# Edge passes of an attention layer in chunks of 32 steps instead of 16, with rings of 64 places and new engine orders

## The reference

```
h = relu(layernorm(x));  x = x + sage(h)      # two layers: mean of h[src] per dst, then dense, log_softmax
h = relu(layernorm(x));  x = x + attention(h) # two layers:
    q, k, v = h@Wq+bq, h@Wk+bk, h@Wv+bv       # 4 heads of 32
    e = edge_weight @ We
    alpha = sum(q[dst] * (k[src] + e)) / sqrt(32)          # per edge and head
    a = softmax of alpha over the edges of one dst
    out = segment_sum((v[src] + e) * a, dst)
    h = h + relu(batchnorm(gate(out, h@Wskip+bskip)))
```

## Time and profile before

| | |
|---|---|
| median of 3 runs | 9833.48 us (9824.3 to 9843.5) |
| profiled execution | 9827.85 us, its span 9826.1 us |
| busy share | POOL 66%, DVE 57%, PE 55%, ACT 30% |
| gathers | 6656, POOL, L537 and L1138 |
| DMA moved | 1053.31 MB, mean 107 GB/s |

### The profile page before, as it was taken

One profiled execution on the slowest core, in us unless ns is written; L12 is line 12 of the kernel. 1 busy time (PEld: TensorE's weight loads), 2 busy tenths in 40 slices (PEclk: granted clock), 3 DMA queues, 4 the chain that ended last, 5 costly groups with the idle time before them and its releaser, 6 DMA issues. The chain is left out here.

```text
span 9826.1 us, 135707 instructions
## 1 busy us (share of the span) xinstructions
PE 5382.9 (55%) x24088; PEld 4490.4 (46%) x24088; DVE 5601.9 (57%) x17532; ACT 2975.7 (30%) x6690; POOL 6499.9 (66%) x6729
## 2 busy tenths in 40 slices
PE   1444444447444444443367677777656777767774
PEld 1333333335333333332156566666525666656663
DVE  4333333332333333334777777777767777777776
ACT  2000000002000000000246666666524666666663
POOL 4777777772577777775067777777605777777770
PEclk8555555558655555555777777777777777777777
DMA  5222222222222222222355555555435555555553
GB/s 118 53 52 53 53 52 53 53 53 76 62 53 53 53 52 53 53 53 56 116 162 161 159 159 159 161 160 161 136 125 165 159 159 154 159 159 160 160 149 105
DMA packets 648320, 1053.31 MB, mean 107 GB/s; under 512 B 287942, under 2 KB 445894, under 8 KB 621528
## 3 DMA queue, kind: packets, MB, share of 16 engines
q0 software_dynamic: 268320, 659.00, 24.7%
q1 hardware_dynamic: 286552, 323.24, 10.6%
q10 hardware_dynamic: 93408, 70.66, 2.2%
HBM read 974.79 MB, written 77.54 MB: 107 GB/s over the span
## 5 line engine op out<-in xcount | busy, mean ns | idle before, releaser
L1138 POOL DMA_INDIRECT conv_kv<-key_value,conv_src x3328 | 3265.7, 981 | 1698.6 <-issue 968.2
L537 POOL DMA_INDIRECT second_msg<-sage_hidden_projected,second_src x1664 | 1586.8, 954 | 749.8 <-issue 506.8
L537 POOL DMA_INDIRECT first_msg<-sage_in,first_src x1664 | 1585.2, 953 | 559.3 <-issue 506.8
L1394 PE MATMUL conv_ps_sums<-conv_pv,conv_sel 128*128 128x136 f32 x6656 | 1511.6, 386 | 396.8 <-DVE conv_pv L1197 209.5
L594 PE MATMUL first_ps_sums<-first_msg,first_sel 128*128 128x129 f32 x3328 | 858.4, 439 | 1258.3 <-DVE first_sel L548 907.6
L594 PE MATMUL second_ps_sums<-second_msg,second_sel 128*128 128x129 f32 x3328 | 858.4, 439 | 1250.4 <-DVE second_sel L548 907.3
L1394 PEld LDWEIGHTS conv_ps_sums<-conv_pv,conv_sel 128*128 128x128 f32 x6656 | 1258.8, 270 | 583.7 <-issue 310.1
L1375 PE MATMUL conv_ps_query<-query_table,conv_selT 128*128 x6656 | 1331.6, 363 | 75.0 <-issue 61.5
L594 PEld LDWEIGHTS first_ps_sums<-first_msg,first_sel 128*128 128x128 f32 x3328 | 745.2, 329 | 1371.4 <-DVE first_sel L548 989.3
L594 PEld LDWEIGHTS second_ps_sums<-second_msg,second_sel 128*128 128x128 f32 x3328 | 745.1, 329 | 1363.8 <-DVE second_sel L548 989.0
L1375 PEld LDWEIGHTS conv_ps_query<-query_table,conv_selT 128*128 128x128 f32 x6656 | 1174.8, 262 | 96.4 <-issue 78.8
(11 more groups left out here) (210 smaller groups left out, 5443.7 us busy)
## 6 DMA issues: line engine op xcount, KB each, us to landing
conv_place<-place_rows SPq DMA_DIRECT2D x208, 1024.0 KB
conv_kv<-key_value,conv_src POOLq DMA_INDIRECT x3328
first_msg<-sage_in,first_src POOLq DMA_INDIRECT x1664, 2.5
second_msg<-sage_hidden_projected,second_src POOLq DMA_INDIRECT x1664, 2.5
key_value<-project_kv ACTq DMA_DIRECT2D x28, 896.0 KB
conv_pen<-run_penalties SPq DMA_DIRECT2D x832, 24.2 KB
project_hT<-conv_in_transposed SPq DMA_DIRECT2D x28, 448.0 KB
combine_hT<-conv_in_transposed SPq DMA_DIRECT2D x28, 448.0 KB
```

The lines of the kernel that those rows point to most:

```text
L537: pool.indirect_dma_start(msg[:, (b % 2) * CH + j, 0:D], None, table, bass.IndirectOffsetOnAxis(ap=src[:, b, j:j + 1], axis=0)).then_inc(g ...
L1138: pool.indirect_dma_start(kv[:, h * CH + j, :], None, t.kv_d, bass.IndirectOffsetOnAxis(ap=src[:, h, j:j + 1], axis=0)).then_inc(gathered[ ...
L1394: last = pe.matmul(sums_of(step), sel[:, h * CH + step, :], pv[:, step, :, :].rearrange("p h w -> p (h w)"), start=True, stop=True)
```

## The change

CH becomes 32: 52 chunks of 8 groups, rings of 64 places, HR = 128 rows in the tiles of the softmax chain. This holds for the `sage_edges` passes too, whose code is not changed otherwise. In `conv_edges`:

- `multiply` writes the products over the keys in `kv`, `weigh` writes over the values in `kv`, and the softmax weights and the weighted edge weights go to the last 8 of the 128 key columns, so that PE's operand of 136 columns is a piece of `kv`. `prod` and `pv` are gone. The order of the 136 columns of the sums changes, and `conv_combine` and `rescaled` (now two operations) with it.
- `away` and `awayT` are gone: ACT works in place in `sel` and `selT`, which are now rings of 4 groups.
- `place` is loaded in four pieces of 512 KB per chunk of 32; `rec` is split into `wd` (weights and dead marks) and `rel` (the node of each edge), each with a load of its own.
- POOL may reuse a place only when PE's sums of it are done (`sums_ready`).
- DVE's order: `stages(a, b)` has first the softmax of the older chunk b, with the scores of three groups of the newer chunk a in its gaps (`fill`), then all eight `weigh` with `rescaled` after the first, then five sections, each with multiply, edge term and score sum of one group of a, and 6 or 7 adds of b. Block numbers are read 16 at a time, twice per chunk. The orders of PE, ACT and SP follow.

```diff
-CH = 16
+CH = 32
+SELG = 4
+NEAR = 3
+DEN = D - 2 * HEADS
+ADDS = (0, 7, 14, 20, 26, CH)
+PAIRS_OF = ((0, 4), (4, 7), (7, 10), (10, 13), (13, KP))
...
                         for k in range(KG):
-                            pool.wait_ge(pv_ready, KG * c + k + 1)
+                            pool.wait_ge(sums_ready, KP * c + 2 * k + 2)
...
+                def scores(a, k):
+                    m = multiply(a, k)
+                    edge_term(a, k)
+                    need(m)
+                    score_sum(a, k)
...
+                    values = slots(h, k)[:, :, D:2 * D].rearrange("p i (h c) -> p i h c", h=HEADS)
+                    dve.tensor_tensor(values, values, bc(slots(h, k)[:, :, DEN:DEN + HEADS], 3, [P, GR, HEADS, C]),
                                       ALU.mult).then_inc(pv_ready, 1)
...
+                def blocks_of(b, half):
+                    c, h, g = b
+                    if half == 0:
+                        dve.wait_ge(blk_in[h], 16 * g + 16)
+                        dve.sem_inc(go_v, 1)
+                    dve.load(regs, blk[0:1, h, half * (CH // 2):(half + 1) * (CH // 2)])
...
+                    at = softmax(b, fill)
+                    weigh(b, 0)
+                    before[0] = rescaled(b, at)
+                    for k in range(1, KG):
+                        weigh(b, k)
+                    for k in range(NEAR, KG):
+                        if a is not None:
+                            m = multiply(a, k)
+                            edge_term(a, k)
+                        lo, hi = ADDS[k - NEAR], ADDS[k - NEAR + 1]
+                        for step in range(lo, hi):
+                            if step == CH // 2:
+                                at = blocks_of(b, 1)
+                            add(step, at)
+                            if step == lo and a is not None:
+                                need(m)
+                                score_sum(a, k)
...
+                    for k in range(NEAR, KG):
+                        if a is not None:
+                            if k == KG // 2:
+                                at = blocks_of(a, 1)
+                            queries(a, k, at)
+                        sums(b, *PAIRS_OF[k - NEAR])
                     if following is not None:
-                        queries(following, 2, at)
-                    return at
+                        queries(following, 0, blocks_of(following, 0))
```

More of the change, by code:

```diff
@@ L1109, in _, with places @@
             def _(sp):
+                flat = t.place_d.rearrange("c n -> (c n)")
+                steps = t.b_d.rearrange("c n -> (c n)")
+                def places(c, h, g, q):
+                    sp.wait_ge(place_used, 4 * c + q + 1)
+                    sp.dma_start(place[:, q % 2, :], flat[bass.ds(c * (CH * P) + q * (2 * GR * P), 2 * GR * P)]
+                                 .partition_broadcast(P)).then_inc(place_in[q % 2], 16)
                 with sp.Fori(0, PAIRS) as g:
@@ new lines, in softmax @@
+                def softmax(b, fill):
+                    c, h, g = b
+                    step = [stp[:, h, :, n] for n in range(HK)]
+                    near = score[:, h, :, :]
+                    dve.wait_ge(q_used, KG * c + KG + 2)
+                    need(chain.n)
+                    m = mark(dve.tensor_tensor(near, near, qwe[:, :, :], ALU.add))
+                    need(m)
+                    dve.tensor_tensor(near, near, bc(wd[:, h, 1, :], 1, [P, HEADS, CH]), ALU.add).then_inc(scored, 1)
+                    fill(0)
@@ L1351, in _, with stages, add, fill @@
-                stages(chunk(PAIRS - 1, 1), chunk(PAIRS - 1, 0), None)
-                stages(None, chunk(PAIRS - 1, 1), None)
+                    dve.sem_inc(wd_used, 1)
+                    return at
+                def stages(a, b):
+                    c, h, g = b
+                    before = [None]
+                    def add(step, at):
+                        j = step // PAIR
+                        if step % PAIR == 0:
+                            dve.wait_ge(sums_ready, KP * c + (j + 1 + 2 * KP))
+                        if step > 0 and step % PAIR == 0:
+                            dve.wait_ge(ps_used, KP * c + (j + 2))
+                        else:
+                            need(before[0])
+                        acc = t.acc[:, bass.ds(at[step % (CH // 2)] * AW, AW)]
+                        ins = dve.tensor_tensor(acc, acc, sums_of(h, step), ALU.add)
+                        if step % PAIR < PAIR - 1:
+                            before[0] = mark(ins)
+                        else:
+                            ins.then_inc(ps_used, 1)
+                    def fill(k):
+                        if a is not None:
+                            scores(a, k)
+                    at = softmax(b, fill)
[13 more added lines that the diff above has]
+                            if step == lo and a is not None:
+                                need(m)
+                                score_sum(a, k)
@@ L1354, in _ @@
+                for k in range(KG):
+                    scores(chunk(0, 0), k)
+                stages(chunk(0, 1), chunk(0, 0))
+                with chain.turns(PAIRS - 1, 2 * (2 * KG + 15 + KP)) as g:
+                    stages(chunk(g + 1, 0), chunk(g, 1))
+                    stages(chunk(g + 1, 1), chunk(g + 1, 0))
+                stages(None, chunk(PAIRS - 1, 1))
             @block.tensor
             def _(pe):
-                pe.sem_inc(q_ready, KG)
+                pe.sem_inc(q_ready, SELG)
@@ L1368, in loaded, with blocks_of @@
                     return [pe.snap(r, min_val=0, max_val=NB - 1) for r in regs]
+                def blocks_of(a, half):
+                    c, h, g = a
+                    if half == 0:
+                        pe.wait_ge(blk_in[h], 16 * g + 16)
+                        pe.sem_inc(go_t, 1)
+                    pe.load(regs, blk[0:1, h, half * (CH // 2):(half + 1) * (CH // 2)])
+                    return loaded()
                 def queries(a, k, at):
@@ L1409, in stages @@
                     pe.wait_ge(scored, c + 1 + 2)
                     pe.sem_inc(go_t, 1)
-                    pe.transpose(rows, score[:, :, :].rearrange("p h t -> p (h t)"), t.ident[:, :]).then_inc(rows_ready, 1)
-                    sums(b, (6,))
+                    pe.transpose(rows, score[:, h, :, :].rearrange("p h t -> p (h t)"), t.ident[:, :]).then_inc(rows_ready, 1)
+                    if a is not None:
+                        queries(a, 1, at)
                     pe.wait_ge(ends_ready, c + 1)
```

363 lines of the change are left out of this document (138 added, 225 removed).

## The result

The changed kernel takes 9773.67 us (9765.26 to 9781.53, 4 runs) where the kernel before takes 9834.67 (9824.3 to 9843.5, 4 runs): a ratio of 0.9939, interval 0.9925 to 0.9952, 61 us faster. A second comparison gave 9775.52 us against 9824.89, 0.9949 (0.9935 to 0.9964). The profiled execution took 9781.53 us, the slowest of its four; its span is 9779.8 us, 46.3 us less than the span before, where the medians differ by 61.

A forecast was written before the change was run, and what follows sets the result against it. The prediction took POOL's gather pace to bound all four passes. Held gathers at -26 us and ends of passes at +26 us, all else 0, summed to no change: 9833 us, range 9775 to 9900.

The forecast's parts named there:

- The frame: All four edge passes: POOL's pace of 1.25 us a gather sets them, 1664 gathers or 2080 us a pass.
- Held gathers: Conv passes: gathers held by DVE operations with two SBUF inputs fall from 120.7 to 95 us, -26 us.
- the distance of 1.815 us: Row of weighs: from a held gather's release to the next start, landing where it just escapes or is caught for 0.5 us.
- Rival A: Conv passes: gathers mostly escape at the seams of the eight weighs, 0.45 us a chunk, -48 us, 9785 us; chance 0.29.
- Ends of passes: Conv passes' ends: the last chunk's work lies open, about +13 us a pass, +26 us for two.
- DVE's turn: DVE's work for 32 steps: 36.5 us, 4 us shorter than POOL's 40.9, so its saving is worth 0.
- rival B: Conv passes: DVE and PE become the bound; a turn of 43 us gives 10080 us, 41.5 us gives +90; chance 0.15.
- Starts: Starts of passes: the first gather's wait for the src load and that load's wait for DVE's clearing both stay, 0.
- SP's queue: SP's loads: same place bytes in half-size pieces, half as many small tables of twice the size, issued early enough, 0.
- the new condition of POOL: POOL's place reuse: `sums_ready` replaces `pv_ready`, yet each place is free 19 to 32 us ahead, 0.
- Sage passes: Sage passes: DVE groups meeting gathers come half as often but behind a 32-register load, between -14 and +14 us, taken as 0.
- Rival C: Conv passes: gathers are caught in step with DVE's weighs, 1.4 us a chunk, +51 us, 9885 us; chance 0.18.

The follow-up runs named there:

- i1: Kernel before, with `weigh` and L548 each reading one input from PSUM and the fourth weigh moved ahead of the last two score operations: 9688.16 us, ratio 0.9864.
- g4: Kernel before, with all four weighs of a chunk in a row at its head, nothing else altered: 9754.55 us, ratio 0.9926.
- g2: Changed kernel, with each score sum of a conv pass done twice, the second into an unread tile: 10053.01 us, ratio 1.023 to the kernel before.
- g1: Changed kernel with nothing altered, run again beside the kernel before on one chip: 9775.52 us, ratio 0.9949.
- g3: Kernel before, with each score sum of a conv pass done twice, the second into an unread tile: 9797.13 us, ratio 0.9971.

## Why the prediction was wrong

*The frame held.* POOL's pace sets the passes: the gathers became 78.1 us shorter and the conv passes 77.4 us; i1 forecast 136 us from lengthened gathers alone and measured 135.

*The step that failed is "Held gathers", -26 us where -78 was measured.* The mechanism was right, its size was not. I had the one catch and the distance of 1.815 us = 3 x 0.604 that puts the next gather on a seam. I then let that gather be "just caught" for a part of the phases, and took the one behind it, 2 x 0.604 = 1.208 against 1.25 us, to start 0.04 us into a weigh and lose 0.5 us. That gave 0.73 us for a row of seven. The row loses 0.18 us. What I didn't know is who gives way at a seam: DVE does, by 0.04 us, and so the next gather meets a seam too. 104 rows x 0.55 us = 57 us, against the 52 by which the term was off (95 forecast, 42.6 measured; the other operations hold gathers for 0.05 us a chunk more than I gave them). The trace of before had this: its 40 gathers within 0.02 us of a weigh's start lost nothing. I didn't look for them, and priced positions at random where the earlier trace rows could have been asked gather by gather. Rival A, at 0.29, was the true one; its 0.45 us a chunk is 0.41 as measured (42.6 / 104).

*Ends of passes, +26:* 38.3 us for 38, and +27.6 in the two gaps behind the conv passes. Right. g4 shows what that costs: 21 us between two kernels with the same gathers.

*DVE's turn, 36.5 us and 4 us of slack:* too short. The slack was 2.0 us, by g2, so the turn is 38.4 us. The first register load stops DVE 1.6 us (ahead of L1257) and not 0.65: the load itself takes 1.10 us in both kernels, but in the kernel before it runs beside two weighs that DVE already has, and here beside nothing. And ahead of L1226, the first operation of each turn of the loop, DVE stops for 3.3 us or so in "issue", 24 times in 1950 us:

```profile
6029.44 0.29 DVE L1226 TENSOR_TENSOR conv_score<-conv_score,conv_qwe 128x128 f32<-128x128 f32 x1 [3.37 <-issue]
```

That is 1.6 us a chunk. The two are more than the 1.9 us that the sum lacks, so other terms of it were too long; they weren't measured one by one. In the kernel before no such row stands, and the instruction queue moved 30 packets, 0.25 MB, where it now moves 428. The records of DVE's sequencer place the stop: it lies between the loop's branch and the next instruction, 3.2 us in the median where the kernel before has 0.23, and in each of the 48 stops of the two passes a packet of the instruction queue starts within the first 2.5 us. This is what rival B's sentence on the doubled loop bodies spoke of; what the Trainium skill says of taken branches (Runtime: NRT & Kernel Launch, section Instruction fetch mechanics) fits, though no run altered the size of the loop alone, so the cause is argued, not shown. At 40.4 us POOL still hid it: rival B didn't come, with 2.0 us to spare where I gave it 4. Its price was 26 us too high besides: I added the longer ends to a turn counted from the forecast, which already had them, so a turn of 43 us gives 10051 us and one of 41.5 us +62.

*Starts, SP's queue, the new condition of POOL, at 0:* right (18.6 us under POOL's new wait are ordinary gaps). *Sage passes, 0 with bounds of 14:* +10.1 and -5.6 us in the first comparison; in g1 they last 2093.5 and 2086.2 us for 2092.0 and 2093.6, so +1.5 and -7.4. Within the bounds.

*Rival C* rested on the second conv pass of before (72 us) as a sign of phases that repeat. g3's 46.4 us there, and a spread of 38 us between runs of before, suggest that it was one draw.

*A row that I misread:* ACT does nothing in a sage pass (0.00 in the earlier trace rows), so only PE and DVE do about twice as much in a conv pass. The conclusion doesn't hang on it.

## What to carry to other kernels

When one engine's pace sets the time and another's operations lengthen it, ask for the position of each meeting and not for a mean: here gathers were lengthened by 121 us with the 832 operations in singles and pairs and by 43 us with them in rows, and moving two lines of the order bought more than rebuilding the pass. (On the chips of 12.3 ms the same two lines cost 494 and 681 us: such an order has to be measured where it is to run.) Better still, take away what makes the lock (an input from PSUM that was there anyway), which was worth 135 us. And when an unseen cost is priced from a handful of rows, look in the trace of before for the case on which the price turns; here the seam was in it 40 times.

## What the runs showed of the hardware

- An operation of DVE with both inputs in SBUF holds a gather only if the gather starts between about 0.03 and 0.565 us after it (of 0.69 us), and holds it until 0.565 us. A gather that starts with the operation passes, and DVE's operation takes 0.72 to 0.73 us for 0.68.
- With one of the inputs in PSUM, at 683 ns for 689, it holds none: no gather of 3328 over 1.0 us in the sage passes. In the conv passes 53 remain, all of which start in a shorter operation (0.22 to 0.41 us) with two inputs in SBUF and are let go after 0.09 to 0.24 us.
- A load of 16 registers takes DVE's sequencer 1.10 us. Behind two queued operations DVE stands idle for 0.7 us of it, behind none for 1.6 us in all.
- With the longer loop body DVE stops for some 3.3 us behind the branch of each turn (78.6 us, 24 times; 0.23 us from branch to instruction in the kernel before), and the instruction queue moves 428 packets for 30.
- Some chips run these kernels at 12.3 ms for 9.8: same instruction times, waits up to 19.6 us put down as "remote". Four groups of runs of six met one, chips 13 and 14. The cause is open.
